# Another order of the same steps in a software-pipelined decoder layer

## The reference

```python
x = x + attn(layernorm(x), Wq, bq, Wk, bk, Wv, bv, Wo, bo)       # 16 heads of 16
x = x + xattn(layernorm(x), ctx, ctx, mask, Wq, ...)             # 77 keys
x = x + ffn(layernorm(x), gamma_x, gamma_slot, slot_embeds, w1, w2)

# ffn:
xn, se = rms_norm(x, gamma_x), rms_norm(slot_embeds, gamma_slot)  # 8 experts x 128 slots
logits = einsum('bsd,etd->bset', xn, se)
dispatch = softmax(logits, axis=1)                                # over tokens
slots = einsum('bsd,bset->betd', xn, dispatch)
processed = gelu(slots @ w1) @ w2                                 # 256 -> 1024 -> 256
combine = softmax(logits.reshape(b, s, e * t), axis=-1)           # over slots
out = einsum('bnd,bsn->bsd', processed.reshape(b, e * t, d), combine)
```

## Time and profile before

| | |
|---|---|
| median of 3 runs | 1773.68 (1773.43 to 1777.49) |
| span of the profiled execution, first to last instruction | 1770.5 |
| the profiled execution's own device time | not recorded apart from its span |
| first step of the loop (`m1.lt.0`) starts | 229.82 |
| first step of FINISH (`m14.lt.0`) starts | 1599.64 |
| TensorE busy | 98% of the span |
| VectorE, ScalarE, POOL busy | 65%, 58%, 25% |

### The profile page before, as it was taken

The page is one execution under the profiler, slowest core; times in us unless marked ns, Lnnn a source line. Parts: engine busy times, 40 slices in busy tenths (PEclk is TensorE's granted clock), DMA queues, the critical chain, the costliest instruction groups (busy, mean ns, idle before and its releaser), DMA issues.

```text
span 1770.5 us, 40859 instructions
## 1 busy us (share of the span) xinstructions
PE 1735.7 (98%) x17306; PEld 1570.7 (89%) x17306; DVE 1158.1 (65%) x2307; ACT 1018.4 (58%) x1775; POOL 439.5 (25%) x354
## 2 busy tenths in 40 slices
PE   8999999999999999999999999999999999999998
PEld 7779798998989888898988989898898988989988
DVE  4656576675867667676666867667576666765453
ACT  4445756566656656656565655656655655655553
POOL 2112122222223122222222313222222313222232
PEclk9999999999999999999999999999999999999999
DMA  5000000000000000000000000000000000000000
GB/s 163 10 1 10 2 10 8 10 8 2 16 1 10 7 10 8 2 16 2 10 8 8 10 2 10 8 10 7 1 16 2 10 8 10 8 1 7 2 7 7
DMA packets 20852, 19.67 MB, mean 11 GB/s; under 512 B 9920, under 2 KB 19776, under 8 KB 20288
## 3 DMA queue, kind: packets, MB, share of 16 engines
q1 hardware_dynamic: 20672, 17.06, 3.5%
HBM read 12.86 MB, written 4.19 MB: 10 GB/s over the span
## 4 chain that ended last, share of the span: by engine, by line
PE 85%; ACT 5%; DVE 4%; issue 4%; POOL 1%; DMA 0%; POOLq 0%; SPq 0%; DVEq 0%; ACTq 0%
PE ps L465 21%; PE ps L466 19%; PE ps L467 19%; PE ps L590 3%; PE ps L573 2%; PE ps L553 2%; PE ps L775 2%; PE ps L700 2%; PE ps L620 2%; PE ps L843 2%; PE ps L665 1%; PE ps L766 1%; POOL h_lo L1446 1%; PE ps L872 1%; ACT L1034 1%
## 5 line engine op out<-in xcount | busy, mean ns | idle before, releaser
L1446 POOL TENSOR_TENSOR h_lo<-h_f,h_hi 128x512 fp32r<-128x512 f32 x256 | 336.9, 1324 | 1052.7 <-DVE h_hi L1329 1052.7
L465 PE MATMUL ps<-sl_hi,w_hi 128*128 128x256 f32 x1024 | 304.9, 298 | 5.4 <-DVE sl_lo L1088 2.9
L465 PE MATMUL ps<-w_hi,h_hi 128*128 128x256 f32 x1024 | 300.9, 294 | 5.5 <-POOL h_lo L1446 5.3
L466 PE MATMUL ps<-w_hi,h_lo 128*128 128x256 f32 x1024 | 290.1, 283 | 0.0
L467 PE MATMUL ps<-w_lo,h_hi 128*128 128x256 f32 x1024 | 289.8, 283 | 0.0
L466 PE MATMUL ps<-sl_hi,w_lo 128*128 128x256 f32 x1024 | 288.8, 282 | 0.0
L467 PE MATMUL ps<-sl_lo,w_hi 128*128 128x256 f32 x1024 | 288.8, 282 | 0.0
L465 PEld LDWEIGHTS ps<-sl_hi,w_hi 128*128 128x128 f32 x1024 | 194.4, 190 | 28.9 <-ACT h_f L1034 14.2
L1329 DVE CAST h_hi<-h_f 128x512 fp32r<-128x512 f32 x256 | 175.4, 691 | 67.1 <-ACT h_f L1034 66.3
L1034 ACT ACTIVATE h_f<-ps 128x512 f32<-128x512 f32 x256 | 151.2, 598 | 104.6 <-PE ps L467 103.6
L465 PEld LDWEIGHTS ps<-w_hi,h_hi 128*128 128x128 f32 x1024 | 196.0, 191 | 15.0 <-POOL h_lo L1446 11.3
(11 more groups left out here) (213 smaller groups left out, 4217.8 us busy)
## 6 DMA issues: line engine op xcount, KB each, us to landing
x<-in_x SPq DMA_DIRECT2D x16, 256.0 KB, 2.7
out<-acc SPq DMA_DIRECT2D x16, 256.0 KB, 2.2
g_w<-in_w SPq DMA_DIRECT2D x2, 1024.0 KB, 12.2
cx<-in_ctxT SPq DMA_DIRECT2D x16, 77.0 KB, 2.0
g_wqk<-in_wqk SPq DMA_DIRECT2D x1, 1024.0 KB, 6.8
g_se<-in_se SPq DMA_DIRECT2D x1, 1024.0 KB, 8.7
biases<-in_bias SPq DMA_DIRECT2D x1, 640.0 KB, 5.1
mk_i<-in_mask SPq DMA_DIRECT2D x16, 38.5 KB
```

The source lines that it names most:

```text
L465: te.matmul(o, lhs[0], rhs[0], start=first, stop=False)
L466: te.matmul(o, lhs[1], rhs[0], start=False, stop=False)
L1446: Q_.tensor_tensor(h_lo[:, part, :], h_f[:, part, :], h_hi[:, part, :].bitcast(f32), ALU.subtract)\
```

## The change

All four strings of `ORDER`, `START` and (but for POOL) `FINISH` are replaced. The steps and the instructions in them stay; only their order changes, and the fill has 150 `idle` units in place of 197 (99 and 51 with batch 0 and 1, where there were 134 and 63). The lists of users of the shared banks, written by hand before, are now derived from TensorE's order; they follow TensorE's order in both kernels. The DMA queue's order is the same. The changed file is one line shorter ahead of the functions, so its line numbers are smaller by one (L886 is L885).

The core of the diff, of one round on TensorE and of the first strings of the fill:

```diff
 ORDER = dict(
     pe="""
-        m.lt.0 l.outer.3.0 d.kv m.dispatch.0 l.outer.3.1 c.xt.1 m.slots.0 l.comb.3 d.xt.2 c.k c.q d.q2 c.v
+        m.lt.0 l.outer.3.0 d.kv m.dispatch.0 l.outer.3.1 c.xt.1 m.slots.0 l.comb.3 c.k d.xt.2 c.q c.v d.q2
         m.hidden.0.0 d.scores2.0 m.hidden.0.1 m.hidden.0.2 d.mt2.0 m.hidden.0.3 m.lt.1 l.combine.3 d.shifted2.0
...
-        m.combine.1 d.oproj2 c.shifted.2 m.dispatch.3 c.tr.0 m.outer.2.0 c.ob.0 c.scores.3 c.pv.2 m.slots.3 m.comb.2
+        c.shifted.2 d.oproj2 m.dispatch.3 m.outer.2.0 c.tr.0 m.slots.3 c.ob.0 c.scores.3 c.pv.2 m.comb.2 m.outer.2.1
...
 START = dict(
     pe="""
-        s0.idle.8 c0.xt.1 s0.idle.18 c0.k c0.q c0.v s0.idle.17 c0.scores.0 s0.idle.10 c0.mt.0 s0.idle.4 c0.shifted.0
+        s0.idle.10 s0.idle.2 c0.xt.1 s0.idle.6 c0.k c0.q c0.v s0.idle.8 s0.idle.8 c0.scores.0 s0.idle.7 s0.idle.4
...
-        s0.idle.5 d0.q2 s0.idle.3 c1.xt.1 d0.scores2.0 s0.idle.1 c1.k d0.mt2.0 c1.q d0.shifted2.0 c1.v s1.idle.2
+        s0.se_transp.1.1 c1.xt.1 d0.scores2.0 c1.k d0.mt2.0 c1.q d0.shifted2.0 c1.v d0.scores2.1 d0.pv2.0 s1.idle.3
...
     act="""
-        c0.xt.1 s0.hi.0 s0.hi.1 c0.k c0.q c0.kh c0.qh s0.hi.2 c0.mh.0 c0.ex.0 s0.se_squares c0.xo.0 c0.mh.1 c0.ex.1
+        s0.hi.0 s0.hi.1 s0.hi.2 c0.xt.1 c0.k c0.q c0.kh c0.qh s0.se_squares c0.mh.0 c0.ex.0 c0.xo.0 c0.mh.1 c0.ex.1
...
     dve="""
-        c0.stats.1 c0.xh.1 c0.xt.1 s0.lo.0 s0.columns s0.lo.1 c0.kd c0.qd c0.v c0.kl c0.qs c0.mx.0 c0.sh.0 c0.mx.1
+        c0.stats.1 s0.lo.0 c0.xh.1 c0.xt.1 s0.columns s0.lo.1 c0.kd c0.qd c0.v c0.kl c0.qs c0.mx.0 c0.sh.0 c0.mx.1
...
     pool="""
-        c0.rstd.1 c0.bias.1 s0.se_scale d0.rstd.2 c1.rstd.1 d0.bias.2 s0.lo.4 d0.rstd.3 m0.hid.0.0 c1.bias.1
-        m0.hid.0.1 m0.hid.0.2 m0.hid.0.3 c2.rstd.1 c2.bias.1 d1.rstd.2 m0.hid.1.0 d1.bias.2 m0.hid.1.1 m0.hid.1.2
+        c0.rstd.1 c0.bias.1 s0.se_scale d0.rstd.2 c1.rstd.1 c1.bias.1 s0.lo.4 d0.bias.2 d0.rstd.3 m0.hid.0.0
+        m0.hid.0.1 m0.hid.0.2 m0.hid.0.3 d1.rstd.2 c2.rstd.1 m0.hid.1.0 m0.hid.1.1 m0.hid.1.2 m0.hid.1.3 m0.hid.2.0
...
-MISC = """
...
+def misc_users():
+
+    for b, kind, step in pe_entries():
+        name, _, k = step.partition(".")
+        if kind != "s" and name in MISC_STEPS:
+            yield f"{'m' if kind == 'l' else kind}{b}.{name}{k if name == 'xt' else '.' + k if k else ''}"
```

More of the change, by code:

```diff
@@ new lines @@
+        m.hidden.1.1 d.scores2.1 m.hidden.1.2 m.hidden.1.3 d.mt2.1 m.lt.2 m.combine.0 c.pv.0 d.shifted2.1 d.tr2.0
+        m.outer.1.0 m.dispatch.2 c.scores.1 d.pv2.1 m.slots.2 m.comb.1 d.ob2.0 m.outer.1.1 c.mt.1 m.hidden.2.0
+        c.shifted.1 d.tr2.1 m.hidden.2.1 c.scores.2 c.pv.1 m.hidden.2.2 d.ob2.1 m.hidden.2.3 m.lt.3 c.mt.2 m.combine.1
+        c.shifted.2 d.oproj2 m.dispatch.3 m.outer.2.0 c.tr.0 m.slots.3 c.ob.0 c.scores.3 c.pv.2 m.comb.2 m.outer.2.1
+        c.mt.3 m.hidden.3.0 c.shifted.3 d.xt.3 m.combine.2 m.hidden.3.1 c.pv.3 m.hidden.3.2 c.tr.1 m.hidden.3.3 c.ob.1
@@ L70 @@
[L70 to L73, removed]
+        m.cm.0 d.mask m.edn.0 c.stats.1 d.stats.2 d.kv c.xh.1 m.ds.0 c.xt.1 d.xh.2 m.row_max l.cb.3 m.sl.0 d.xt.2 c.qd
@@ new lines @@
+        d0.mt2.1 s1.idle.5 d0.shifted2.1 d0.tr2.0 s1.idle.3 d0.ob2.0 s1.idle.1 c1.scores.0 d0.pv2.1 s1.idle.2 d0.tr2.1
+        s1.idle.4 c1.mt.0 s1.idle.3 d0.ob2.1 c1.shifted.0 d0.oproj2 c1.scores.1 c1.pv.0 s1.idle.6 c1.mt.1 s1.idle.4
+        c1.shifted.1 s1.idle.4 s1.idle.1 d0.xt.3 s1.idle.6 d0.logits.0 d0.logits.1 d0.logits.2 d0.logits.3 s1.idle.2
+        c1.scores.2 c1.pv.1 m0.lt.0 s1.idle.3 s1.idle.1 c1.mt.2 s1.idle.2 s1.idle.1 c1.shifted.2 c1.tr.0 m0.dispatch.0
+        c1.ob.0 c1.scores.3 c1.pv.2 m0.slots.0 c1.mt.3 m0.hidden.0.0 m0.hidden.0.1 c1.shifted.3 d1.kv m0.hidden.0.2
@@ new lines @@
+        c1.pv.3 c1.tr.1 m0.hidden.0.3 c1.ob.1 m0.lt.1 c1.oproj m0.outer.0.0 m0.dispatch.1 m0.outer.0.1 c2.xt.1
+        m0.slots.1 m0.comb.0 c2.k c2.q m0.hidden.1.0 m0.hidden.1.1 c2.v d1.xt.2 m0.hidden.1.2 m0.hidden.1.3
+        m0.combine.0 c2.scores.0 m0.lt.2 d1.q2 m0.outer.1.0 c2.mt.0 m0.dispatch.2 c2.shifted.0 m0.slots.2 m0.comb.1
+        d1.scores2.0 m0.outer.1.1 m0.hidden.2.0 d1.mt2.0 m0.hidden.2.1 d1.shifted2.0 m0.hidden.2.2 c2.pv.0
+        d1.scores2.1 d1.pv2.0 d1.mt2.1 m0.combine.1 d1.shifted2.1 m0.lt.3 d1.tr2.0 d1.pv2.1 c2.scores.1 m0.hidden.2.3
@@ L179 @@
+        m-1.hid.3.1 m-1.pr.2 m-1.hid.3.2 m-1.hid.3.3 m-1.acc.2 m-1.cb.3 m-1.pr.3 m-1.acc.3 m-1.finish
     """,
```

180 lines of the change are left out of this document (83 added, 97 removed).

## The result

The changed kernel takes 1781.29 us, median of 9 runs (1778.31 to 1787.4), against 1775.45 for the kernel before in the same session: a ratio of 1.0035, 95% interval 1.0022 to 1.0047. It is slower by about a third of a per cent.

What follows compares the result with a forecast made beforehand. TensorE, busy 98% of the span, was taken as the bound. Terms 4.5 + 3.0 − 1.0 − 0.5 − 4.0 + 0.5 = +2.5 on the 1770.5 span gave 1773.0; plus 3.2 for the median, 1776.2 us, range 1766 to 1784.

Steps and rivals of the forecast that it cites:

- the fill only: Rival: in the fill the clock falls in both places (+6) and the loop wins nothing; 1783 us, chance 0.16.
- The first wait of the fill: Start of the kernel: ScalarE waits for the third weight's data ahead of batch 0's tile, delaying `c0.k`; +4.5 us.
- The clock: Batch 0's k and q matmuls, perhaps again between 53 and 66: half clock after idling; +3 us, bounds 0 to +6.
- The wait removed: Fillers of batch 1 behind `c1.v` no longer wait for VectorE; −1.0 us, between 0 and −1.4.
- The rest of the fill: 112 to 230: POOL's new order may free `qs` and `kl`, against a later `m0.cm.0`; −0.5 us, bounds −2.1 and +2.4.
- The loop: 13 rounds: shorter waits and fewer transpose pairs against small new waits, −0.3 us a round; −4.0, bounds −13 and +3.
- the wait that I feared at `m.hidden.3.2`: In each loop round, TensorE waits for the Gelu behind Exp, tile copy and table load; 0 to 0.3, taken +0.1 us.
- The slower rival: One new loop wait at `m.hidden.3.2`, 0.6 us a round, +8 in place of −4; 1784 us, chance 0.14.
- The end: After the loop: `m.hidden.1.0` loses `d.shifted2.0` as cover for its wait for `cb_lo`; +0.5 us, bounds 0 and +1.6.

## Why the prediction came out as it did

The forecast was 1776.2 in a range of 1766 to 1784, with slower by over 0.3% at 0.36 and within 0.3% at 0.44. The measured +5.8 us (1781.29 against 1775.45) lies in the range and just over that bound, and its interval (1.0022 to 1.0047) reaches to both sides of it. It is nearest to the rival that I called the fill only, at 0.16: the clock falls and the loop wins nothing, 1783. That the time lies in the range is in part luck. The forecast added +2.5 to the profiled span, and the profiled span grew by 12.8; the error of 10.3 shrank to 5.1 since I had carried over that the median stands 3.2 above the span, and in the changed kernel it stands 2.0 below it.

*The first wait of the fill* was sized at +4.5 and measured +4.2, +4.3 when put into the kernel before. The mechanism was as written: the DMA lands at 14.2, ScalarE, VectorE and TensorE follow. What the prediction did not mention is that `lo.0` ahead of `c0.xh.1` makes `c0.k` 1.0 late even without that wait, and that 11.99 was set by the fillers of the kernel before, 0.9 behind the last input.

*The clock* was +3 (0 to +6) and measured 5.3: 1.5 at k and q (the clock fell at 17 and rose at 20, so half of what I took) and 3.8 between `c0.oproj` and `c1.v`, which I had called cheap since "the small steps there wait for others". That was wrong: with the clock held, the stretch was 3.8 shorter. The idle time ahead of k and q was not the "over 6 us" of the prediction either: the transposes, which I had done before 10, came at 10.72 behind `lo.0`, and the idle time was 2.53 ahead of them and 2.15 behind the fillers. The Trainium skill (TensorE: Matmul & The Clock Gate, part 1) says that half rate is the default and activity releases it. By that rule a fill with fewer fillers can lose the clock, and the three places agree (0.50, 0.65 and 0.50 in the windows above).

*The wait removed,* −1.0, was exact: `c1.v` to `d0.scores2.1` takes 2.13 in the changed kernel. *The rest of the fill,* −0.5, was +0.7 from `d0.scores2.1` to the loop. What I had counted on came: `qs` and `kl` of the third batch take 1.28 and 1.21 in place of 2.31 and 2.32. But from `m0.outer.0.0` to the loop that gave only 0.3, and between `d0.logits.0` and `m0.outer.0.0` the new order loses 1.1, with TensorE idle for 0.96 ahead of `c1.mt.3` and 0.73 ahead of `c1.tr.1`, for which I had no term.

*The loop* is where the forecast failed: −4.0 was taken, −0.3 measured. A gain that I had under-sized and a loss that I had not seen nearly cancel in it: −7.4 and +7.1 (1369.5 against 1362.4). Without the moved step the new order gains 7.4, 0.57 a round. Of it 0.26 is at `m.outer.0.0` (I had 0.20: the chain of POOL does start earlier), 0.25 at `m.dispatch.3` and `c.tr.0` together (0.16), 0.10 at `m.dispatch.3`'s own wait, which I had said would stay (counted with `c.shifted.2` and `d.oproj2`, 3.05 became 2.95), and the wait that I feared at `m.hidden.3.2` is nowhere. Against it stands what I did not see at all: `d.stats.2` had stood between the issue of x and the step that reads it; in the new order VectorE comes to that step at about 3.4 in the round, before the load has landed (3.5 to 4.5), and does `d.stats.2` only behind it. The step of the working that failed is its list of the loop's new waits ("New ones: `d.mt2.0` ... and `m.hidden.3.2`"), which lacks `c.xt.1`; that cost 6.8 with the new `ORDER` alone and took the loop's whole gain. The slower rival had the right form (one new wait in the loop, in place of its gain) at the wrong place. Its sum was wrong as well: +8 in place of the −4 gives 1788, and the 1784 holds only if the wait comes on top of the −4.

*The end* was +0.5 (0 to +1.6). Up to `m15.lt.0` it is 1.6, of which `cb_lo` is 0.8 more than before and the rest a wait for `acc` at `m14.outer.1.0` that I had not looked for. The other 1.7 of the profiled execution lie behind `m15.lt.0`: there the changed kernel takes 88.66 for 85.69 with the same `FINISH` at full clock, so 3.0 went to the clock, and the kernel before had lost 1.5 in the same way.

*The sum:* 4.2 + 5.3 − 1.0 + 0.7 + 0.6 (other steps between `c0.v` and `c1.v`, by subtraction) − 0.3 + 3.3 = 12.8, the difference of the two profiled spans. The medians differ by 5.8 only. This profiled execution was one of the slower ones (1785.1, 3.8 above its median), and that of the kernel before a fast one (a run's time is 1.8 above its span, so 1772.3, 3.2 below its median). The nine runs spread over 9.1 us, those of before over 4.1, and in the changed kernel's runs the time rises with the share of half clock, from 1778.31 at a mean clock of 0.998 to 1787.4 at 0.991. What stays open is how often each of the places falls, since each profile shows one execution, and so which part of the 5.3 belongs in the median.
